# The last attention of a four-layer model: scores issued further ahead, last copies on another engine, value products taken one step later

## What is computed

```python
q = (x @ Wq + bq).reshape(1, B * N, H, hd)          # B*N = 2048 rows, H = 16 heads of hd = 16
kv = (cond @ Wkv + bkv).reshape(1, -1, 2, H, hd)
...
q = _fq_sym(q * scale, axis=-1)                     # 8 bit, one step for each row and head
k = _fq_sym(k, axis=-1)
v = _fq_sym(v, axis=2)                              # one step for each column, over all 2048 rows
attn = softmax(einsum('bhqd,bhkd->bhqk', q, k))
attn = _fq_unsigned(attn, axis=-1)                  # 8 bit, one step for each row
out = einsum('bhqk,bhkd->bhqd', attn, v)
```

## Time and profile before

| | us |
|---|---|
| three runs | 2674.13, 2672.82, 2669.72 (median 2672.82) |
| the profiled execution | 2669.46 |
| its span, first to last instruction | 2667.7 |
| of it, qkv3 | about 1502 to 1642 |
| of it, attend3 | about 1642 to 2309 |
| VectorE busy over the span | 1801.6 (68%) |
| TensorE busy over the span | 2376.5 (89%) |
| ScalarE busy over the span | 1555.3 (58%) |

### The profile page before, as it was taken

The page is one execution under the profiler, slowest core; times in us unless marked ns, Lnnn a source line. Parts: engine busy times, 40 slices in busy tenths (PEclk is TensorE's granted clock), DMA queues, the critical chain, the costliest instruction groups (busy, mean ns, idle before and its releaser), DMA issues. The chain is left out here.

```text
span 2667.7 us, 49543 instructions
## 1 busy us (share of the span) xinstructions
PE 2376.5 (89%) x18506; PEld 1596.7 (60%) x18514; DVE 1801.6 (68%) x4468; ACT 1555.3 (58%) x2793; POOL 606.4 (23%) x658
## 2 busy tenths in 40 slices
PE   6977999999999978679889777999999999899999
PEld 5655666666566644367656565555555555566666
DVE  6857777675434339767567677999999999633321
ACT  4544665665333337634444346999999999622322
POOL 2214334332222113333123114111111111121111
PEclk9989999999999989999999988999999999999999
DMA  4120000000200021021100233566677666400000
GB/s 148 45 90 5 13 9 9 19 5 7 85 24 24 9 91 52 17 82 41 45 22 22 66 104 127 100 121 121 114 119 127 114 118 116 82 16 13 20 5 12
DMA packets 318716, 157.24 MB, mean 59 GB/s; under 512 B 265216, under 2 KB 314384, under 8 KB 317456
## 3 DMA queue, kind: packets, MB, share of 16 engines
q1 hardware_dynamic: 318480, 154.09, 25.0%
HBM read 66.48 MB, written 23.07 MB: 34 GB/s over the span
## 5 line engine op out<-in xcount | busy, mean ns | idle before, releaser
L2736 DVE CUSTOM_DVE_ANT_0 arena<-psum,attend_zero,queries_step 128x1024 f32<-128x1024 f32 x512 | 633.9, 1282 | 16.5 <-PE psum L2785 11.9
L2712 ACT ACTIVATE attend_ex<-arena,attend_mx 128x2048 uint16<-128x2048 f32 x256 | 512.8, 2003 | 10.0 <-issue 8.4
L1515 PE MATMUL psum<-arena,moe_tokT 128*128 128x512 f32 (+2 forms) x896 | 360.6, 547 | 2.7 <-DVE moe_h L1402 2.6
L2785 PE MATMUL psum<-keys_turned,queries_ahead 96*128 96x512 bf16 x1024 | 306.9, 381 | 3.4 <-PEq L2285 2.0
L2810 PEld LDWEIGHTS psum<-values,attend_pw 128*128 128x128 f16 x4096 | 175.2, 96 | 136.2 <-issue 19.7
L1515 PEld LDWEIGHTS psum<-arena,moe_tokT 128*128 128x128 f32 x896 | 166.0, 191 | 138.6 <-issue 120.7
L1402 DVE TENSOR_TENSOR moe_h<-moe_sg,psum 128x512 f32<-128x512 f32 (+1 forms) x112 | 69.9, 625 | 262.9 <-PE psum L1515 258.1
L1249 ACT ACTIVATE moe_sg<-psum 128x512 f32<-128x512 f32 (+1 forms) x112 | 61.3, 548 | 291.3 <-PE psum L1515 287.0
L2697 POOL TENSOR_SCALAR attend_mx<-attend_mx 128x1 f32<-128x1 f32 x256 | 75.1, 293 | 584.2 <-DVE attend_mx L2736 584.2
L2795 PE MATMUL psum<-ident_b,attend_ex 128*128 128x128 bf16 x2128 | 165.9, 221 | 46.7 <-ACT attend_ex L2712 26.6
L2795 PEld LDWEIGHTS psum<-ident_b,attend_ex 128*128 128x128 bf16 x2128 | 122.8, 98 | 123.2 <-ACT attend_ex L2712 116.6
(11 more groups left out here) (452 smaller groups left out, 4658.5 us busy)
## 6 DMA issues: line engine op xcount, KB each, us to landing
residual<-stored_rows SPq DMA_DIRECT2D x48, 128.0 KB, 1.7
queries_turned<-queries_rows SPq DMA_DIRECT2D x16, 384.0 KB, 3.1
queries_ahead<-queries_turned SPq DMA_DIRECT2D x16, 384.0 KB, 4.1
arena<-in_moe SPq DMA_DIRECT2D x1, 5704.0 KB, 18.4
arena<-in_gqa SPq DMA_DIRECT2D x1, 5440.0 KB, 17.6
arena<-in_moe SPq DMA_DIRECT2D x1, 4360.0 KB, 13.8
xatt_ct<-in_ctx_T SPq DMA_DIRECT2D x32, 128.0 KB, 2.3
residual<-stored_rows SPq DMA_DIRECT2D x16, 256.0 KB, 2.1
```

Source lines behind the costliest of these rows:

```text
L1515: last = nc.tensor.matmul(bank[:, q % 2, 0:size], tokT[:, i % 2, j, ic], wt[:, ic, at:at + size], start=ic == 0, stop=ic == DC - 1)
L2712: nc.scalar.activation(ex[:, u % ER:u % ER + 2], kept[:, u % KR:u % KR + 2], ACT.Exp, bias=mx[:, t % 2, h, 2:3], scale=-1.0, accum_out=sum ...
L2736: nc.vector.tensor_tensor_reduce(kept[:, u % KR], S[:, u % 2], zero[:].to_broadcast([P, UK]), steps[:, t, h:h + 1], 3.0e38, ALU.add, ALU.m ...
L2785: last = nc.tensor.matmul(S[:, u % 2, b * 512:(b + 1) * 512], qt[:, t % 2, h * P:(h + 1) * P], KT[:, c:c + 4, h // 2], start=True, stop=True)
```

## The change

In `qkv3` VectorE's step takes the value products of the step before (tiles 2i - 2 and 2i - 1) straight behind `bias`; `stats` and `norm` move behind `key_values` and the first `rest`; `widest` comes in steps 2, 4, 6 and 8. ScalarE copies the turned queries before the turned keys and does both `place_q` before the second cast. TensorE turns queries before keys and has three `keep_busy` matmuls in place of five. In `attend3` scores are issued seven units ahead (`AHEAD`); a one-element exp at ScalarE's start has the table of exp loaded there; of the last four copies out of PSUM, those of units 508, 509 and 511 go to VectorE with a semaphore of their own (`tail`); and TensorE's last units are written out, without `keep_clock`.

```diff
--- before.py
+++ after.py
@@ -2437,13 +2437,13 @@
 
             act.wait_ge(s["padded"], 1)
             for i in range(-2, B + 1):
+                at(turned_q, i - 1)
                 at(turned_k, i - 1)
-                at(turned_q, i - 1)
                 if 0 <= i < B:
                     cast_k(i, 0, "kq", "k_hi")
                     place_q(i, 0)
+                    place_q(i, 1)
                     cast_k(i, 1, "k_r1", "k_mid")
-                    place_q(i, 1)
                     cast_k(i, 2, "k_r2", "k_lo")
                 at(turned_x, i + 2)
 
@@ -2522,21 +2522,23 @@
 
             stats(0)
             for i in range(-2, B):
-                at(bias, i)
+                if i < 0:
+                    norm(i + 2)
+                    stats(i + 3)
+                    continue
+                bias(i)
+                at(values, 2 * i - 2)
+                at(values, 2 * i - 1)
+                quantise(i)
+                key_values(i)
+                at(stats, i + 3)
+                if i in (2, 4, 6, 8):
+                    widest(i // 2 - 1)
+                rest(i, 0, "k_hi", "k_r1")
                 at(norm, i + 2)
-                at(stats, i + 3)
-                at(quantise, i)
-                at(key_values, i)
-                at(values, 2 * i)
-                at(values, 2 * i + 1)
-                if i >= 0:
-                    rest(i, 0, "k_hi", "k_r1")
-                if i in (1, 3, 5, 7):
-                    widest(i // 2)
                 if i == 9:
                     value_steps()
-                if i >= 0:
-                    rest(i, 1, "k_mid", "k_r2")
+                rest(i, 1, "k_mid", "k_r2")
 
         @block.tensor
         def _(pe):
@@ -2589,9 +2591,9 @@
                 if 1 <= i <= B:
                     if i >= 3:
                         pe.wait_ge(s["qT"], 2 * i - 4)
-                    keep_busy(nc, k, 2 * ((i - 1) % 2), 5)
+                    keep_busy(nc, k, 2 * ((i - 1) % 2), 3)
+                at(turn_q, i - 1)
                 at(turn_k, i - 1)
-                at(turn_q, i - 1)
                 at(queries_keys, i + 1)
                 at(values, 2 * i)
                 at(values, 2 * i + 1)
@@ -2609,7 +2611,7 @@
     UN = 2 * NH
     NU = B * UN
     KR, TR, ER = 8, 2, 8
-    LAG = 6
+    AHEAD, LAG = 7, 6
     EVERY = 1
     LN255 = 5.541263545158426
     with ExitStack() as ctx:
@@ -2618,7 +2620,7 @@
 
         s = semaphores(nc, k, "attend3_", """
             weights_next q_loaded0 q_loaded1 o_stored0 o_stored1
-            zeroed scores kept bias exped turned evacuated landed0 landed1 landed2 landed3
+            zeroed scores kept bias exped turned evacuated tail landed0 landed1 landed2 landed3
             attended row_recip probs_step scaled o_done""")
         S = k["psum"][:, 0:4, :].rearrange("p (u b) c -> p u (b c)", b=2)
         TPW = k["psum"][:, 4:4 + TR, :]
@@ -2626,6 +2628,7 @@
         IDLE = k["psum"][:, 6]
         O = k["psum"][:, 7, 0:D]
         zero = sb("zero", [P, 1])
+        warm = sb("warm", [P, 1])
         kept = arena[:, 0:KR * UK].rearrange("p (r c) -> p r c", r=KR)
         mx = sb("mx", [P, 2, NH, 3])
         sums = sb("sums", [P, 2, NH])
@@ -2643,13 +2646,20 @@
             return u % 2 == 1 and u // 2 % EVERY == EVERY - 1 and 2 * ER <= u < NU - 4
 
         turned_ahead = [sum(not by_dma(v) for v in range(u)) for u in range(NU)]
+        turned_units = [u for u in range(NU) if not by_dma(u)]
         landed_ahead = [sum(by_dma(v) for v in range(u % ER, u, ER)) for u in range(NU)]
 
         def counts_read(eng, u):
             eng.wait_ge(s[f"landed{u // 2 % 4}"], (landed_ahead[u] + 1) * 16) if by_dma(u) else eng.wait_ge(s["turned"], turned_ahead[u] + 1)
 
+
+        tail = (NU - 4, NU - 3, NU - 1)
+
+        def evacuated(eng, u):
+            eng.wait_ge(s["tail"], tail.index(u) + 1) if u in tail else eng.wait_ge(s["evacuated"], turned_ahead[u] + 1 - sum(v < u for v in tail))
+
         def turned_kept(eng, u):
-            eng.wait_ge(s[f"landed{u // 2 % 4}"], (landed_ahead[u] + 1) * 16) if by_dma(u) else eng.wait_ge(s["evacuated"], turned_ahead[u] + 1)
+            eng.wait_ge(s[f"landed{u // 2 % 4}"], (landed_ahead[u] + 1) * 16) if by_dma(u) else evacuated(eng, u)
 
         @block.sync
         def _(sp):
@@ -2716,11 +2726,13 @@
                 act.wait_ge(s["turned"], turned_ahead[u] + 1)
                 nc.scalar.copy(pw[:, u % ER], TPW[:, turned_ahead[u] % TR]).then_inc(s["evacuated"], 1)
 
+            act.wait_ge(s["zeroed"], 1)
+            nc.scalar.activation(warm[:], zero[:], ACT.Exp)
             for n in range(NU // 2 + 1):
                 if n < NU // 2:
                     exp(n)
                 for u in range(2 * n - 2, 2 * n):
-                    if u >= 0 and not by_dma(u):
+                    if u >= 0 and not by_dma(u) and u not in tail:
                         evacuate(u)
 
         @block.vector
@@ -2755,6 +2767,10 @@
             def scale_columns(t):
                 dve.wait_ge(s["scaled"], t + 1)
                 nc.vector.tensor_tensor(o[:, t % 2], o[:, t % 2], v_step[:], ALU.mult).then_inc(s["o_done"], 1)
+
+            def evacuate(u):
+                dve.wait_ge(s["turned"], turned_ahead[u] + 1)
+                nc.vector.tensor_copy(pw[:, u % ER], TPW[:, turned_ahead[u] % TR]).then_inc(s["tail"], 1)
 
             for u in range(NU):
                 t, at = u // UN, u % UN
@@ -2766,7 +2782,10 @@
                         scale_rows(t - 1)
                     if at == LAG + 5:
                         scale_columns(t - 1)
+            evacuate(NU - 4)
+            evacuate(NU - 3)
             row_steps(B - 1)
+            evacuate(NU - 1)
             scale_rows(B - 1)
             scale_columns(B - 1)
 
@@ -2790,7 +2809,7 @@
                 rank = turned_ahead[u]
                 pe.wait_ge(s["exped"], u + 1)
                 if rank >= TR:
-                    pe.wait_ge(s["evacuated"], rank - TR + 1)
+                    evacuated(pe, turned_units[rank - TR])
                 for c in range(UC):
                     last = nc.tensor.transpose(TP[:, rank % TR, c], counts[u % ER][:, c * P:(c + 1) * P], k["ident_b"][:])
                 last.then_inc(s["turned"], 1)
@@ -2811,17 +2830,22 @@
                                             start=kc == 0, stop=kc == B - 1)
                 last.then_inc(s["attended"], 1)
 
-            for u in range(5):
+            for u in range(AHEAD):
                 score(u)
-            for u in range(NU + LAG):
-                if u < NU and not by_dma(u):
+            for u in range(NU - 2):
+                if not by_dma(u):
                     turn(u)
-                if u + 5 < NU:
-                    score(u + 5)
+                if u + AHEAD < NU:
+                    score(u + AHEAD)
                 if u >= LAG:
                     attend(u - LAG)
-                if u < NU:
-                    keep_clock()
+                keep_clock()
+            for u in range(NU - 2 - LAG, NU - 4):
+                attend(u)
+            turn(NU - 2)
+            turn(NU - 1)
+            for u in range(NU - 4, NU):
+                attend(u)
 
 
 def mask_bit(nc, k, x_in, x_out, ctx_T, ctx_rows, masks, arena, load_next, hand, ternary):
```

## The result

| | us |
|---|---|
| before, median of 7 runs | 2671.24 (2667.95 to 2679.10) |
| after, median of 7 runs | 2660.74 (2654.01 to 2664.57) |
| ratio after / before | 0.9956, 95% interval 0.9941 to 0.9970 |
| forecast | 2650.0 (2640 to 2659) |
| profiled execution after | 2654.01, span 2652.2, mean granted clock 0.969 |

The change gains 10.5 us by the medians. The forecast had 22, and the median lies 1.7 us above its range. The profiled execution is the shortest of the seven; the other six took 2658.9 to 2664.6, with mean granted clocks of 0.963 to 0.966 where the profiled one has 0.969.

What follows compares the result with a forecast made beforehand. A chain of waits bounds the projections, nearly full VectorE and ScalarE the attention. Gains of 17.2 and 5 us, together 22.2, take 2669.5 to 2647.3; the median, 3.4 higher, was given as 2650 us, range 2640 to 2659.

Steps and rivals of the forecast that it cites:

- Projections: First section, qkv3: value products a step later and VectorE's other moves remove waits; gain 17.2 us, range 12 to 19.5.
- The loop through the value products: Projections: rest, cast, turn_k, turn_q, products, values, rest was said to set the pace; its 1.00 us wait goes.
- Fill, table, tail: Attention's start and end: fill idle falls from 6.7 to 3.4 us, early exp table 0 of 1.30, last copies 0.6 net.
- The last sum: End of the forecast: 2647.3 us for the profiled execution, median 3.4 higher, given as 2650 us.
- Body gain 1.4: Attention from the 20th to the last maximum: 18.2 us of small waits go, 16.8 come back; gain 1.4 us.
- The stall: Attention, before scale_rows behind maximum 10: VectorE waits for an attend behind score 12; 1.02 us in each of 15 tiles.
- rival 1: Projections: TensorE loses its clock with fewer dummies, value steps run slow; 45 us, 2695 us; chance 4%.
- Rival 5: Projections: the loop through values is not the pace-setter, only 5 of the 17 us arrive; 2662 us; chance 4%.
- Rival 3: Attention gains nothing, the stall being longer or met twice a tile; 2655 us; chance 14%.
- Rival 2: Attention: no new stall at scale_rows, body gain about 15 us; 2636 us; chance 7%.
- Rival 4: GpSimd ends the projections, its code load stretching once the data are there; +4 us, 2654 us; chance 12%.
- its detour: Projections: GpSimd's all-reduce starts 6.09 us after it is free, next instruction 7.77 after its end; 15 us.

Runs made afterwards that it cites:

- c2: Changed kernel, six scores ahead, projections as before except VectorE's values and widest a step later: 2642.66 us, ratio 0.9878.
- b3: Changed kernel, six scores ahead, VectorE's old order in the projections; TensorE's turns and three dummies, ScalarE's placements stay changed: 2645.67 us, ratio 0.9902.
- c1: Changed kernel, seven ahead, plus six dummy matmuls a tile ahead of the scores of iterations 6 and 7, behind the turn: 2651.80 us, ratio 0.9914.
- c3: Changed kernel, six scores ahead, projections as before except VectorE's stats and norm moved: 2658.92 us, ratio 0.9943.
- a1: Changed kernel with scores issued six ahead in place of seven, nothing else different: 2634.94 us, ratio 0.9848.
- a2: Changed kernel, seven ahead kept, with scale_rows and scale_columns each one maximum later: 2635.01 us, ratio 0.9853.
- b1: Changed kernel plus six dummy matmuls a tile behind the attends of iterations 4 and 5, four of them ahead of the stalled score: 2662.01 us, ratio 0.9959.
- a3: Changed projections (qkv3) with the attention (attend3) of the kernel before: 2656.34 us, ratio 0.9937.

## Why the prediction was wrong

**Projections: right.** 18.4 us where 17.2 were forecast (17.9 if the sum's own end, the last copy, is taken); steps of 6.20 and 8.42 where 6.25 and 8.45 stood; 8.10 for step 9 instead of 8.5. The reason was right but incomplete. The loop through the value products was one of two things that had to go together, since the move alone gives 10.3 of the 18.4 (c2). And the turn order, with the placements and the dummies, which I priced at nothing of their own, gives 9.6 alone (b3).

**Fill, table, tail: right in size.** From the first to the 20th maximum 26.85 us for 29.57: 2.7 gained, where I had 3.3. End 5.45 us behind the last exp, forecast 5.3; ScalarE trails the last maximum by 0.9 us more, forecast 0.8, and VectorE's copies take 0.69 us each, as bounded by the bias addition of that shape. The last sum, 2647.3 + 3.4, is 2650.7 and not 2650; that changes nothing here. The timeline of VectorE at the end:

```profile
2286.49 0.69 DVE L2773 COPY attend_pw<-psum 128x512 f32<-128x512 f32 x1 [1.72 <-PE psum L2814]
2287.36 0.69 DVE L2773 COPY attend_pw<-psum 128x512 f32<-128x512 f32 x1 [0.17 <-PE psum L2814]
...
2289.47 0.69 DVE L2773 COPY attend_pw<-psum 128x512 f32<-128x512 f32 x1 [0.73 <-PE psum L2814]
2290.67 0.42 DVE L2764 TENSOR_TENSOR stored_rows<-psum,attend_tot 128x256 f32<-128x256 f32 x1 [0.51 <-PE psum L2829]
```

**The step that failed: "Body gain 1.4".** From the 20th to the last maximum 1.4 us were to be gained, and 5.5 were lost in the profiled execution: 6.9 off. The stall was where I put it, as long as I said (0.94 idle is 1.02 from the end of the maximum to `scale_rows`), in as many tiles, and the undisturbed period is 40.66 against 40.7 forecast. But I summed it as time of VectorE alone, and put what it does to TensorE at nothing. While VectorE stalls no maximum ends, and one stalled maximum later TensorE idles for it; I asked of the projections what such idles do to the clock (rival 1) and did not ask it of the attention, where the clock had been 1.00. There it cost 6.5 us in the profiled execution and some 11 by the ratios of the change and c1. With the idles filled (c1) the stall stays, the body takes 626.4 us, 0.9 less than before, and the ratio is 0.9914, where the forecast was 2650.0 / 2672.8 = 0.9915. So the clock accounts for the error; that the last digit nearly agrees is luck, for the projections came out better than forecast and fill and body a little worse. Rival 5 (2662) is nearest to the median of 2660.7, but its mechanism is out: the projections gained all they were to gain. Rival 3 (the attention gains nothing, 2655) had the right section, and its mechanism, a stall longer or met twice, was not the one; the rows behind the stall show the clock instead. None of the five had the loss of clock in the attention.

**Rival 1** had the right mechanism in the wrong section. In the changed projections TensorE does fall to half clock behind idles of 2.54 and 3.44 us:

```profile
1557.51 0.44 PE L2552 MATMUL psum<-ident,qkv_xn 128*128 128x128 f32 x2 [2.54 <-DVE qkv_xn L2466]
...
1560.55 1.02 PE L2587 MATMUL psum<-ident_b,qkv_Kp 128*96 128x128 bf16 x8
...
1572.51 0.69 PE L2552 MATMUL psum<-ident,qkv_xn 128*128 128x128 f32 x2 [3.44 <-DVE qkv_xn L2466]
```

The keys' turn takes 1.02 us there, 0.61 at full clock. It costs little: 0.29 us at L2504 and a step 8 of 8.80 for 8.42. c3 suggests that it can cost more. The rule of the Trainium skill's "TensorE: Matmul & The Clock Gate" (Why this matters for your kernels), that long idle gaps bring the clock down, pointed at the steps with `widest`, and the trace agrees there. It does not point at the attention, whose idles of 1.09 and 0.52 us are among the short ones, and yet the clock fell behind them in five tiles of 14. The measurement decides.

**Rival 2** (no new stall, a body gain of about 15, 2636) is what a1 and a2 reach: 2635, with 16.6 gained from the 20th to the last maximum in a1. **Rival 4**: GpSimd did not end the projections; its last rounding started at 1617.01, 5 us before ScalarE's last copy ended. Of its detour the first 6 us can hide, as c2 shows.

**What stays open:** why the clock falls in some tiles and not in others with the same idles, and how many tiles it takes in the longer executions. Of those there is no trace; their lower mean clocks (0.963 to 0.966 for 0.969) fit more of them. What makes the ninth tile longer by 0.35 us in every kernel wasn't tried.

## What to carry to other kernels

When work is issued further ahead, walk the queue of the engine that issues it and ask what each instruction behind the new one was waiting to deliver. Here the seventh score ahead put an attend behind a maximum, and the operation that wanted the attend stood right behind that maximum; six ahead, or that operation one place later, takes the 0.94 us stall out of each tile, and the ratio is 0.9848 in place of 0.9956. Price a stall twice: the time of the engine that waits, and what TensorE's clock does next if TensorE idles because of it. A few dummy matmuls in that idle are a cheap test of the second, if they stand behind the turn and not ahead of the instruction that the stall waits for.

## What the hardware did that I had not expected

- Idles of 1.09 and 0.52 us, in a stretch in which TensorE was busy for 585.6 of 633 us, were followed by half clock in five tiles of 14; 0.66 and 0.52 (b1) in two; 0.83 to 1.03 and 0.31 in one (a3) or in none (before); with idles of up to 0.5 us (c1, a2; a1 has one of 0.8) the clock stayed at 1.00. In the projections before, an idle of 2.59 us was followed by a turn at full clock.
- The 6 us of GpSimd ahead of the all-reduce run before its data are there (c2). Behind it GpSimd's next instruction came 6.97 us after its end in c2 and 7.77 before.
- At the start of the attention TensorE runs at half clock, before and after the change. A score of 1.03 us costs nothing there in itself, since they still start every 1.20 to 1.22 us, the maxima's pace.
